# Gated cross-attention and FFN block on one core: zero-filled 128-row key stacks in two halves, one buffer for both normalised blocks, residual rows loaded twice, and a new order

## What is computed

```python
dots / (qn[..., :, None] * kn[..., None, :])          # cosine_sim
mixed = cw * cosine_sim + vw * cov_component + ww * var_component
out = jnp.einsum('hqnm,hqmd->hqnd', mixed, f_v)
...
x = x + jnp.tanh(g_xattn[0]) * _L0_xattn_ref(_layernorm(x, axis=-1), ctx_1024, ctx_1024, ...)
...
scores = jnp.einsum('bqd,bkd->bkq', q, k) / jnp.sqrt(jnp.asarray(D, x.dtype))
attn = jax.nn.softmax(scores, axis=-1)
out = jnp.einsum('bkq,bqv->bkv', attn, v)
...
z = z @ Wo
z = _l2_normalize(z)
z = z @ Wff
z = _l2_normalize(z)
z = jax.nn.gelu(z, approximate=False)
...
x = x + jnp.tanh(g_ffn[0]) * _L0_ffn_ref(_layernorm(x, axis=-1), ...)
```

## Time and profile before

| what | us |
|---|---|
| median of three runs | 1537.54 |
| the profiled execution, its own time | 1532.33 |
| its span, first to last instruction | 1530.6 |
| busy: TensorE | 1366.8 (89%) |
| busy: VectorE | 1225.1 (80%) |
| busy: ScalarE | 1026.1 (67%) |
| busy: GpSimd | 443.2 (29%) |

### The profile page before, as it was taken

The page is one execution under the profiler, slowest core; times in us unless marked ns, Lnnn a source line. Parts: engine busy times, 40 slices in busy tenths (PEclk is TensorE's granted clock), DMA queues, the critical chain, the costliest instruction groups (busy, mean ns, idle before and its releaser), DMA issues.

```text
span 1530.6 us, 34938 instructions
## 1 busy us (share of the span) xinstructions
PE 1366.8 (89%) x10624; PEld 810.9 (53%) x10624; DVE 1225.1 (80%) x3180; ACT 1026.1 (67%) x3326; POOL 443.2 (29%) x279
## 2 busy tenths in 40 slices
PE   4997587899999999999999999999999989999865
PEld 2655464555555555555555556464655555555421
DVE  5878766778788897978788878887879798897844
ACT  5564223677767686767777767777777767686766
POOL 1441342324141414141323223242424141414100
PEclk9999799899999999999999999999999999999956
DMA  8430115234352617080808071624334352616050
GB/s 255 136 98 17 40 30 82 63 60 81 66 90 57 100 44 112 16 140 16 140 16 140 17 117 39 83 73 71 85 63 77 66 90 54 103 43 101 24 87 14
DMA packets 125732, 115.10 MB, mean 75 GB/s; under 512 B 8024, under 2 KB 123376, under 8 KB 125680
## 3 DMA queue, kind: packets, MB, share of 16 engines
q1 hardware_dynamic: 125696, 114.66, 38.8%
HBM read 78.40 MB, written 25.32 MB: 68 GB/s over the span
## 4 chain that ended last, share of the span: by engine, by line
PE 29%; DVE 27%; issue 13%; DMA 7%; ACT 7%; SPq 4%; DVEq 1%; POOL 0%; ACTq 0%; POOLq 0%
PE work L749 7%; DVE nm L1440 7%; PE work L751 7%; PE work L750 7%; DMA qstack<-parts 6%; ACT prob L1249 5%; PE score L1164 3%; SPq L1052 3%; PE attended L1176 2%; PE work L1083 2%; DVE vsp L1454 2%; DVE mixed L1398 2%; DMA parts<-kl 1%; DVE zz L1420 1%; DVE l2s L1413 1%
## 5 line engine op out<-in xcount | busy, mean ns | idle before, releaser
L1249 ACT ACTIVATE prob<-score,nm 128x256 f32<-128x256 f32 x1024 | 473.8, 480 | 119.0 <-DVE nm L1440 114.0
L1440 DVE TENSOR_REDUCE nm<-score 128x2 f32<-128x512 f32 x512 | 336.3, 683 | 29.1 <-PE score L1164 28.3
L1164 PE MATMUL score<-qstack,kstack 64*128 64x256 f16 x1024 | 183.5, 280 | 39.0 <-DMA qstack<-parts 20.9
L1249 ACT ACTIVATION_READ_ACCUMULATOR prob<-score,nm 128x1 f32 x1024 | 217.2, 212 | 0.0
L1374 DVE BATCH_NORM_STATS2 qst<-work 128x6 f32<-128x128 f32 x512 | 111.0, 284 | 68.6 <-PE work L751 67.3
L1176 PE MATMUL attended<-prob,vsp 128*32 128x256 f32 x2048 | 143.6, 400 | 22.4 <-DVE vsp L1454 22.4
L1164 PEld LDWEIGHTS score<-qstack,kstack 64*128 64x128 f16 x1024 | 58.8, 95 | 172.4 <-ACT prob L1249 92.6
L1313 POOL TENSOR_TENSOR mixed<-mixed,tmp 128x616 f32<-128x616 f32 x64 | 95.7, 1496 | 177.3 <-DVE mixed L1398 173.7
L1293 POOL TENSOR_TENSOR rq<-qft,mhalf 128x32 f32<-128x32 f32 x16 | 87.0, 5437 | 141.4 <-DVEq L1381 141.4
L1300 POOL TENSOR_TENSOR kTl<-khat,kTh 128x462 f16<-128x462 f32 (+1 forms) x48 | 46.3, 966 | 246.5 <-ACT kTh L1207 246.5
L749 PE MATMUL work<-woutTh,fvph 128*128 128x256 f16 x384 | 106.3, 277 | 0.0
(11 more groups left out here) (291 smaller groups left out, 3564.4 us busy)
## 6 DMA issues: line engine op xcount, KB each, us to landing
krows<-kstat SPq DMA_DIRECT2D x32, 616.0 KB, 5.7
kstack<-parts SPq DMA_DIRECT2D x128, 128.0 KB, 7.9
qstack<-parts SPq DMA_DIRECT2D x128, 128.0 KB, 8.4
s_xin<-in_x SPq DMA_DIRECT2D x8, 1024.0 KB, 5.9
xin<-in_x SPq DMA_DIRECT2D x16, 512.0 KB, 7.4
x<-x2S SPq DMA_DIRECT2D x16, 512.0 KB, 5.3
out<-zb SPq DMA_DIRECT2D x16, 512.0 KB, 5.1
parts<-qh SPq DMA_DIRECT2D x16, 256.0 KB, 2.2
```

The source lines that it names most:

```text
L1164: last = nc.tensor.matmul(sc[n % SC][:, jj * NQ:(jj + 1) * NQ], stack["k"][64 * e:64 * e + 64, j, b2 * NQ + k * P:b2 * NQ + (k + 1) * P], ...
L1249: nc.scalar.activation(prob[:, g % PG, k, u % 4, :], sc[n % SC][:, jj * NQ:(jj + 1) * NQ], ACT.Exp, bias=nm[:, u:u + 1], accum_out=sums[:, ...
L1440: nc.vector.tensor_reduce(nm[:, 2 * n:2 * n + 2], sc[n % SC][:, :].rearrange("p (u q) -> p u q", q=NQ), AX.X, ALU.max, negate=True).then_i ...
```

## The change

A score matmul takes all 128 rows: kstack gets a dimension e, and the 64 rows that belong to the other e are zero, filled once at the start; qstack is read whole. The stacks are read back in two halves, `back0` for the first batch of the pair (scores 0 to 15), `back1` for the second, each with 16 transfers of 256 columns and its own semaphore; `back0` waits only for the first half of the scores of the pair before. z and zz share one buffer, norm, for which z waits for the transposes of zz two pairs back and ln2 for those of z. x2S is filled by a second load of the rows (`ldy`), the bias is added in place, and xb as a buffer is gone; ldx no longer waits for xb. SP starts when all four memsets are done. And `ORDER` is a new sequence.

```diff
-xb G0 G0.h G1 G2 G1.h G0.l G2.h G1.l G3 ldr G2.l G4 qs1 G3.h ldx V0 G4.h S0 V0.h G3.l S1 qpow S2 G4.l G5 M0 V1 G5.h
+G0 qs1 G1 G0.h V0 G1.h G0.l qpow S0 G1.l V0.h G2 M0 G3 G2.h V0.l S1 ldr G3.h S2 G2.l G4 X0 G3.l G5 M1 G4.h V1 G5.h
...
-    xin, xb, zz = w["xin"], sb("xb", [P, PT, DIM]), sb("zz", [P, PT, DIM])
-    z, xTf = sb("z", [P, PT, DIM]), sb("xTf", [P, PR])
+    xin, xTf = w["xin"], sb("xTf", [P, PR])
+    norm = sb("norm", [P, PT, DIM])
...
-    stack = {a: sb(a + "stack", [P, FH // 2, PR], F16) for a in "qk"}
+    qstack, kstack = sb("qstack", [P, FH // 2, PR], F16), sb("kstack", [P, 2, FH // 2, PR], F16)
...
                     sp_wait(z_ready, a)
-                    sp_wait(xb_ready, a)
                     sp.dma_start(xin[:], x_rows[bass.ds(a * PR, PR), :].rearrange("(t p) d -> p t d", p=P)).then_inc(x_ready, 16)
+                elif step == "ldy":
+
+                    sp_wait(zz_ready, a)
+                    sp_wait(x2_in, a * 16)
+                    sp.dma_start(x2S[:], x_rows[bass.ds(a * PR, PR), :].rearrange("(t p) d -> p t d", p=P)).then_inc(y_in, 16)
...
-                elif step == "back":
-
-                    sp_wait(parts_stored, a * 64 + 64)
-                    sp_wait(sc_ready, a * SCORES + START)
+                elif step in ("back0", "back1"):
+
+                    b2 = int(step[-1])
+                    cols = slice(b2 * NQ, (b2 + 1) * NQ)
+                    if b2 == 0:
+                        sp_wait(parts_stored, a * 64 + 64)
+                    sp_wait(sc_ready, a * SCORES - (1 - b2) * SCORES // 2 + SC_CREDIT)
                     for c in range(4):
                         for e in range(2):
-                            for name, n in (("k", 2 + c // 2), ("q", c % 2)):
-                                src = parts[n].rearrange("(q e d) n -> e d q n", e=2, d=FD)[e]
-                                sp.dma_start(stack[name][64 * e + FD * c:64 * e + FD * (c + 1), :, :],
-                                             src).then_inc(stack_in, 16)
+                            rows = slice(64 * e + FD * c, 64 * e + FD * (c + 1))
+                            for dst, n in ((kstack[rows, e, :, cols], 2 + c // 2), (qstack[rows, :, cols], c % 2)):
+                                src = parts[n].rearrange("(q e d) n -> e d q n", e=2, d=FD)[e][:, :, cols]
+                                sp.dma_start(dst, src).then_inc(stack_in[b2], 16)
...
+            sp_wait(init, 4)
             run(sp, a_part, b_part)
...
-                    if n == 0:
-                        pe.wait_ge(stack_in, b * 256 + 256 + START)
+                    if n % (SCORES // 2) == 0:
+                        pe.wait_ge(stack_in[b2], b * 256 + 256 + START)
...
-                                                stack["k"][64 * e:64 * e + 64, j, b2 * NQ + k * P:b2 * NQ + (k + 1) * P],
-                                                stack["q"][64 * e:64 * e + 64, j, b2 * NQ:(b2 + 1) * NQ],
+                                                kstack[:, e, j, b2 * NQ + k * P:b2 * NQ + (k + 1) * P],
+                                                qstack[:, j, b2 * NQ:(b2 + 1) * NQ],
...
             nc.gpsimd.memset(vsp[:], 0.0).then_inc(init, 1)
+            nc.gpsimd.memset(kstack[:], 0.0).then_inc(init, 1)
...
-                    pool.wait_ge(x_ready, a * 16 + 16)
-                    pool.wait_ge(v2_ready, a)
-                    nc.gpsimd.tensor_tensor(xb[:], xin[:], bc(w["tb"][:].unsqueeze(1), [P, PT, DIM]),
+                    pool.wait_ge(y_in, a * 16 + 16)
+                    nc.gpsimd.tensor_tensor(x2S[:], x2S[:], bc(w["tb"][:].unsqueeze(1), [P, PT, DIM]),
                                             ALU.add).then_inc(xb_ready, 1)
...
+                    if not (isinstance(a, int) and a == 0):
+
+                        wait_filled(dve, a - 2, "zz0", "zz1")
...
+                    wait_filled(dve, a + 1, "zT0", "zT1")
```

More of the change, by code:

```diff
@@ L814 @@
[L814 to L818, removed]
@@ L819 @@
-kh2 L3 q1.o O2 pv0.v O3 O2. q2 O3. q3 F1 q2.o pv1 q3.o kl2 F2 q4 pv1.v q5 q4.o F3 q6 q5.o q7 q6.o q7.o F4 out res
+G0 qs1 G1 G0.h V0 G1.h G0.l qpow S0 G1.l V0.h G2 M0 G3 G2.h V0.l S1 ldr G3.h S2 G2.l G4 X0 G3.l G5 M1 G4.h V1 G5.h
+G4.l X1 G5.l M2 S3 V1.h d0 M3 X2 S4 qs2 d1 V1.l X3 M4 S5 V2 ldy d0.o X4 M5 ldx S6 d2 R0 X5 S7 d1.o P0 M6 x0 V2.h M7 X6
+S8 d3 V2.l M8 X7 V3 d2.o d3.o X8 x1 S9 V3.h S10 M9 V4 M10 X9 V3.l S11 R1 V4.h S12 m0 M11 xb m1 m0.h V4.l P1 m1.h m0.l
+X10 d4 m1.l X11 M12 m2 S13 d4.o d5 X12 M13 S14 d5.o d6 m2.h R2 E0 X13 S15 m2.l x2 P2 M14 M15 X14 d7 d6.o X15 V5 d7.o
@@ new lines @@
+L0 S16 x3 V5.h S17 S18 y0 V5.l M16 M17 X16 M18 X17 R3 ldk z X18 S19 m3 m4 m3.h M19 S20 P3 y0.o X19 m3.l m5 m4.h S21
+M20 S22 m5.h fk0 m4.l X20 m5.l M21 zT0 fk0.h S23 M22 y1 E1 X21 L1 fk0.l zT0.h R4 fk0.k zT0.f M23 X22 zT0.l zT1 kh0
+y1.o O0 X23 kl0 ln1 zT1.h S24 fk1 O0. M24 S25 lpow fk1.h P4 M25 zT1.f fk1.l O1 X24 ln2 X25 S26 fk1.k S27 zz0 O1. R5
+zz1 M26 S28 zz0.h P5 M27 zz1.h zz0.l X26 fk2 zz1.l X27 S29 M28 pk0 M29 kh1 zT1.l fk2.h S30 X28 pq0 fk2.l kl1 fk2.k
+pk0.h M30 X29 S31 pk1 pk0.l X30 M31 R6 pq1 pq0.h X31 pq0.l P6 pk1.h R7 pq1.h pk1.l P7 E2 pq1.l L2 q0 parts E3 L3 O2
@@ L820 @@
+q0.o O3 O2. kh2 pv0 O3. kl2 back0 q1 F1 pv0.v q2 q1.o F2 q3 q4 q2.o F3 q3.o q5 q4.o q6 q5.o back1 q7 q6.o F4 pv1 q7.o
+pv1.v out res
 """.split()
@@ L822 @@
 A_INDEX = {name: k for k, name in enumerate(CHUNKS)}
+FIRST_PROJECTION = min(("pq0", "pk0", "pv0"), key=A_INDEX.get)
 WORK_USES = [len(range(s, len(CHUNKS), WORK)) for s in range(WORK)]
@@ L1006, in _ @@
         def _(sp):
-            for waited in (stack_in, ob_ready, vs_ready, sc_ready, stored):
+            for waited in (*stack_in, ob_ready, vs_ready, stored):
                 sp.sem_inc(waited, START)
+            sp.sem_inc(sc_ready, SC_CREDIT)
             sp.sem_inc(exp_done, EXP_CREDIT)
@@ L1079, in a_part @@
                 if kind in ("zT", "zz"):
-                    src = z if kind == "zT" else zz
                     pe.wait_ge(z_ready if kind == "zT" else zz_ready, a + 1)
                     for t in range(PT):
-                        last = nc.tensor.transpose(bk[:, t * P:(t + 1) * P], src[:, t, c * P:(c + 1) * P], ident[:])
+                        last = nc.tensor.transpose(bk[:, t * P:(t + 1) * P], norm[:, t, c * P:(c + 1) * P], ident[:])
                 elif kind == "fk":
@@ L1136, in a_part @@
                 elif kind in ("pq", "pk"):
-                    if e == "pq0":
+                    if e == FIRST_PROJECTION:
                         wait_drained(pe, a, "zz0", "zz1")
@@ L1142, in a_part @@
                 elif kind == "pv":
+                    if e == FIRST_PROJECTION:
+                        wait_drained(pe, a, "zz0", "zz1")
                     for r in range(2):
@@ L1418, in a_part @@
                     dve.wait_ge(r2_ready, a + 1)
+                    wait_filled(dve, a + 1, "zT0", "zT1")
                     for t in range(PT):
-                        last = nc.vector.tensor_scalar(zz[:, t, :], x2S[:, t, :], l2m[:, t, 0:1], l2r[:, t:t + 1],
+                        last = nc.vector.tensor_scalar(norm[:, t, :], x2S[:, t, :], l2m[:, t, 0:1], l2r[:, t:t + 1],
                                                        ALU.subtract, ALU.mult)
```

17 lines of the change are left out of this document (8 added, 9 removed).

## The result

| | before | after |
|---|---|---|
| median, us (4 runs each, same chip) | 1538.12 (1536.1 to 1543.83) | 1498.69 (1497.51 to 1501.03) |
| ratio, 95% interval | | 0.9752 [0.973, 0.9773] |
| profiled execution, its span | 1532.33, 1530.6 | 1498.44, 1496.7 |
| busy: TensorE | 1366.8 | 1318.1 |
| busy: VectorE | 1225.1 | 1179.0 |

What follows compares the result with a forecast made beforehand. TensorE's path bounds the 80.5 us turn: 68.8 work, 5.5 shape changes, 6.2 waits. Terms -60.2, -7.0, -7.0, +7.5 sum to -66.7 from 1530.6, 1463.9; with 1.7 and 5.2 added, 1471 us, range 1440 to 1505.

Steps and rivals of the forecast that it cites:

- 128-row scores: TensorE's score matmuls: 14 shape changes a turn instead of 55, 0.10 us each, taking 4.1 us from its path.
- the rival of exposed loads: Each of 64 score matmuls shows its 95 ns weight load, 6.1 us a turn: turn 82.5, total 1565; chance 0.02.
- The rival by which the shape costs nothing: The 0.1 us belongs to the tile or its semaphores, so the turn stays: 1535 us; chance 0.04.
- Halves: Stack read-back before the first score: 1 MB in 10.4 us instead of 2 MB in 20.7; above 12 signals wrong.
- the rival of packets: 512-byte packets keep a stack DMA's time, 20.7 us a half: ring 98 us, total near 1790; chance 0.07.
- The ring: Last projection through store, read-back, krows and mixing to m0, 39.7 us, then to the last projection: closes at 77.1 us.
- P2's wait: TensorE's 1.14 us wait for vsp at P2, slowed by GpSimd's tmp; half of it was counted as saved.
- The turn: One steady pipeline turn takes 76.2 us, 4.3 less than the 80.5 before; 14 turns give -60.2.
- The start: SP waits for all memsets, so the first q matmul comes at 193.3 instead of 185.77: +7.5 us, between 0 and 12.
- The last pair: Last turn's first score: chain 10.3 us shorter, some 3 us more work ahead of it: -7 us.
- VectorE takes over: VectorE's 68.8 us become 90% of the turn; new waits of 2.3 us give 78.5 and 1503; chance 0.20.
- Nothing else in the way: krows arrives early and both waits vanish: turns of 74 us, total 1440; chance 0.17.

Runs made afterwards that it cites:

- experiment 1: Changed kernel with score matmuls back on 64 rows, stacks, halves and order kept: 1498.23 us, ratio 0.9755 to the kernel before.
- experiment 3: Changed kernel with the second krows load issued ahead of the store of the parts and score matmuls on 64 rows: 1483.68 us, ratio 0.966 to the kernel before.
- experiment 7: Changed kernel with the stacks read back whole, 16 transfers of 1024-byte packets ahead of the first score: 1570.13 us, ratio 1.0199 to the kernel before.
- Experiment 2: Changed kernel with the second krows load moved on SP's queue ahead of the store of the parts: 1453.81 us, ratio 0.9444 to the kernel before.
- experiment 5: Changed kernel with GpSimd's x2 addition waiting for VectorE's vsp of R2, krows left in place: 1466.36 us, ratio 0.9532 to the kernel before.
- experiment 6: Changed kernel with sixteen useless matmuls of 256 columns ahead of m0's wait for mixed: 1477.23 us, ratio 0.9621 to the kernel before.
- experiment 9: Changed kernel with kstack's memset moved behind kl2 of the first pair, SP waiting for it at back0: 1473.53 us, ratio 0.9588 to the kernel before.
- experiment 8: Changed kernel with the order of the kernel before, apart from steps that must move: 1606.51 us, ratio 1.0448 to the kernel before.
- experiment 4: Changed kernel with krows loaded early and GpSimd's x2 addition waiting for VectorE's vsp of R2: 1438.12 us, ratio 0.9364 to the kernel before.
- experiment 10: Changed kernel with krows loaded early, x2 behind R2's vsp and kstack's zeros late: 1426.59 us, ratio 0.9286 to the kernel before.

## Why the prediction was half right

**128-row scores: right as a cost, not as a gain here.** The rows show the changes gone, and weight loads of full rows stay hidden (98 ns each, under a spacing of 0.109 us), so the rival of exposed loads is out. The step failed where it took 4.1 us from the turn by itself: as long as krows sets m0's time, what TensorE saves it waits (experiment 1), and afterwards 1.6 of 4.2 us shows in the turn (experiment 3). Of the other 2.6, 1.4 is seen as smaller waits; the rest wasn't followed up. The rival by which the shape costs nothing is out, though experiment 1 alone would have spoken for it.

**Halves: right in kind, a half takes 12 us and not 10.4.** The forecast halved 20.7 us, which run from the first issue to the first score. To the same point a half takes 12.5 us in the last pair (1429.54 to 1442.04; 19.2 before), and in the middle turns its last transfer lands 11.4 to 12.8 us behind the first issue, 12.1 in the mean. (Half of the 4096 packets have ended after 10.0 us, but they need not all be of the first half.) That is past the 12 us that the prediction named as a sign of being wrong, and it cost nothing in the middle turns: 4.1 + 4.7 + 12.1 = 20.9 us behind the last projection, where TensorE comes to the score after 22.4. Packets of 512 bytes took 81 ns in the mean where those of 1024 took 134, and all of them land in 21.7 us where 20.2 stood: twice as many packets cost some 7%, not 100%, and the rival of packets is out. Experiment 7 shows that the change lives from the halves.

**The ring: right in kind, 1.2 us short.** Forecast from the last projection to m0: 3.3 to the store, 4.7 to the read-back, 20.7 + 5.0 to the first tmp, 6.0 to m0, 39.7 in all. Measured in the same terms, as means of the middle turns: 4.08 + 4.69 + 26.06 + 6.12 = 40.95. Most of the 1.25 us between them is the store, 0.8 us later, because on VectorE R6, R7 and one more split of a projection now stand ahead of the last split, which ends at 720.46 in the turn shown, 3.5 us behind the last projection, where it was 2.8 before. Experiment 2 confirms that this ring bound the turn.

**P2's wait: the step that failed.** "I count on half of it; it is in the 76.2." It didn't shrink: 1.25 us after, 1.14 before. The new order keeps most of the instructions apart (the mean of vsp fell from 0.67 to 0.48 us), but not the one for which TensorE waits: x2's addition became ready with R2's vsp. With it forced behind vsp the turn is 75.9 (experiment 5), where the forecast had 76.0 for the ring without P2's wait, and the time is 1466; the sum agrees, but its parts are 40.6 + 35.3 where 39.7 + 36.3 was forecast.

**The clock: not in the prediction at all.** I priced a wait at its own length. A wait of 1.9 to 3.6 us at m0 also drops the granted clock to 1.2 GHz, in ten of fourteen turns, for the work behind it: P1 at up to 1.94 us. That is 1.5 us a turn, 21 us (experiment 6).

**The turn, added up.** From m0 to the last projection the forecast had 33.8 us of work and 3.6 of waits, 37.4, and 37.4 was measured. That is luck: at full clock the stretch takes 36.1 (experiment 6), so the waits there are 1.3 us smaller than taken, and the low clock, at nothing in the forecast, puts 1.3 back. The miss against 76.2 is elsewhere: the ring as forecast closed at 77.1, and I took 0.9 less, counting on P2; the other 1.2 is the way from the last projection to m0. 76.2 + 0.9 + 1.2 = 78.3, the measured turn. Without the clock it would have been 76.8.

**The start: too small.** +7.5 forecast, +10.4 measured at the first q matmul and +13 at the first G step. krows is later as worked out, but I had the memset hold only SP. It also held VectorE: 8.22 us for the four instructions of the normalisation, of which the second alone takes 7.08, against 1.53 without it (experiment 9), so that the transposes and xTl came late as well. The first pair's score wait fell by 4.1 us, near the 4.9 forecast; the sum of start and first pair is +4.7 instead of +0.5.

**The last pair.** -4.8 instead of -7: its score waits 10.20 us where 8.50 stood. The step that was mis-sized is the half again: the last projection to the score got 6.6 us shorter (26.9 to 20.3) and not 10.3. The 3 us of steps moved ahead of m0 came as forecast, and m0 to the last projection gave 1.2 that the forecast hadn't.

**xb and norm: right.** No wait in the changed kernel points to either; experiment 8 shows the price of norm in another order.

**VectorE takes over: no.** It has 64.3 us in a turn, and 67 to 68 in the same window of 78.2 us in experiments 2, 4 and 10, which holds more than one of their turns; the turn got shorter with repairs that take no work from it. This rival's time, 1503, is near the measured one for another reason.

**Nothing else in the way: not in this kernel, but in experiment 4.** The rival had both waits gone, turns of 74 us and 1440. With krows early and P2's wait at 0.30 us the turn is 74.0 and the time 1438.

## What to carry to other kernels

Close the ring of transfers and steps before adding up what an engine saves: while a load sets the turn, the engine's savings come back as waiting, and the repair may be one line on the queue (45 us here). Price a wait of TensorE with the work behind it, which may run at half clock, and look at the granted clock of the window; if it can't be removed, filling it may pay. When instructions of VectorE and GpSimd are to be kept apart, look at the one whose wait is on the path, since a better mean says nothing of it.

## What the runs showed of the hardware

Useless matmuls in a wait made the kernel faster: 16 of them, 1.75 us by their spacing of 0.109, in each turn, saved 21 us in 1499.

A memset on GpSimd holds VectorE: a copy of 128x8 took 5.77 us beside the memsets of fvph and fvpl (it ends at 176.68, they at 176.66), and four instructions of 128x256 took 8.22 us beside kstack's against 1.53 without it. With GpSimd's additions it is vsp that is held, 0.29 to 1.48 us. The Trainium skill ("SBUF — State Buffer", Who interferes with whom) says that the two engines share a pair of ports as an exclusive lock for a whole instruction, for VectorE's two-port modes and, against a GpSimd instruction that reads SBUF, for two inputs in SBUF. The trace agrees: copy and normalisation are held by memset, and vsp, with two inputs, by additions.

Transfers into 16 partitions are bound by bytes more than by packets: from the first issue to the last landing 2 MB took 21.7 us as 4096 packets of 512 bytes in the changed kernel, and 20.2 as 2048 of 1024 before (20.0 in experiment 7).
